# The sixteen-head stage gets its turned tokens by VectorE, DRAM and small loads instead of TensorE

## The reference

```python
y = x.reshape(b, t, nh, hs).transpose(0, 2, 1, 3)        # nh = 16 heads of hs = 16 features
scores = jnp.einsum('bhtk,bhsk->bhts', y, y) / math.sqrt(hs)
attn = jax.nn.softmax(scores, axis=-1)
o = jnp.einsum('bhts,bsc->bhtc', attn, x)                # every head sums the whole 256-feature tokens
o = o.transpose(0, 2, 1, 3).reshape(b, t, nh * c)
return o @ weight
```

## Time and profile before

| what | value |
|---|---|
| median of 3 runs | 3955.74 us (3955.32 to 3961.43) |
| profiled execution, first to last instruction | 3959.9 us |
| TensorE busy in it | 3751.7 us (95%) |
| VectorE, ScalarE, GpSimd busy | 67%, 57%, 55% |
| chain that ended last | 86% TensorE, 6% VectorE, 3% issue |
| sixteen-head stage | about 1373 us to 2670 us of the span |

### The profile page before, as it was taken

How to read it: one execution, slowest core, us unless ns; L and a number is a source line. 1 busy time by engine, 2 the same in 40 slices (tenths; PEclk the granted TensorE clock), 3 DMA queues, 4 the chain that set the end, 5 groups by cost and what they waited for, 6 DMA issues and landing times.

```text
span 3959.9 us, 75575 instructions
## 1 busy us (share of the span) xinstructions
PE 3751.7 (95%) x23552; PEld 3069.5 (78%) x23552; DVE 2649.7 (67%) x7350; ACT 2237.8 (57%) x5232; POOL 2192.4 (55%) x2179
## 2 busy tenths in 40 slices
PE   4999999999999799999999999998999999999997
PEld 3777777777777688888888888886777777777776
DVE  6677777777777465555555555656777777767774
ACT  2666665567656455444444444445656765567564
POOL 3465565555555355555555555654555555555553
PEclk8999999999999899999999999999999999999999
DMA  4000001110010100000000010001010011100110
GB/s 142 16 31 28 19 19 53 48 36 24 30 31 29 46 28 22 1 17 7 12 17 2 17 44 1 17 1 52 20 35 22 19 41 50 39 30 24 34 32 25
DMA packets 119063, 114.72 MB, mean 29 GB/s; under 512 B 13181, under 2 KB 116233, under 8 KB 118793
## 3 DMA queue, kind: packets, MB, share of 16 engines
q1 hardware_dynamic: 118792, 111.44, 8.9%
HBM read 73.69 MB, written 29.36 MB: 26 GB/s over the span
## 4 chain that ended last, share of the span: by engine, by line
PE 86%; DVE 6%; issue 3%; ACT 2%; POOL 1%; DMA 1%; DVEq 0%; SPq 0%; ACTq 0%; POOLq 0%
PE psum L1366 21%; PE psum L1367 20%; PE psum L1368 20%; PE psum L1480 6%; PE psum L1490 5%; PE psum L1510 4%; PE psum L1469 3%; PE psum L1615 3%; PE psum L1563 1%; DVE probs L1065 1%; PE psum L1446 1%; PE psum L1427 1%; DVE turned_sin L1031 1%; DVE nT_lo L1127 1%; DVE ssq L1038 1%
## 5 line engine op out<-in xcount | busy, mean ns | idle before, releaser
L685 POOL TENSOR_TENSOR ge_lo<-ge,ge_hi 128x512 fp32r<-128x512 f32 x512 | 716.8, 1403 | 541.2 <-PE psum L1368 311.3
L885 ACT ACTIVATE ge<-psum 128x512 f32<-128x512 f32 x512 | 306.3, 598 | 623.7 <-PE psum L1615 611.8
L645 POOL TENSOR_SCALAR probs<-probs,rz 128x256 f32<-128x256 f32 (+1 forms) x1024 | 446.1, 456 | 354.6 <-DVE rz L1079 354.6
L1256 DVE CAST ge_hi<-ge 128x512 fp32r<-128x512 f32 x512 | 245.2, 480 | 537.5 <-ACT ge L885 531.4
L791 ACT ACTIVATE probs<-probs,nb,rq 128x256 f32<-128x256 f32 (+1 forms) x1024 | 575.1, 564 | 20.2 <-DVE nb L1073 17.1
L1065 DVE CUSTOM_DVE_ANT_0 probs<-psum,mask 128x256 f32<-128x256 f32 (+1 forms) x1024 | 339.3, 387 | 255.0 <-PE psum L1480 200.2
L627 POOL TENSOR_TENSOR rinv<-ssq,minus_half 128x16 f32<-128x16 f32 x124 | 376.1, 3033 | 126.6 <-DVE ssq L1042 123.2
L655 POOL TENSOR_TENSOR hid_lo<-gate,hid_hi 128x512 fp32r<-128x512 f32 x160 | 208.2, 1301 | 320.7 <-ACT hid_hi L823 320.7
L1366 PE MATMUL psum<-wqkv_hi,hT_hi 128*128 128x512 f32 x768 | 319.0, 415 | 5.9 <-DVE hT_lo L1016 3.4
L772 ACT ACTIVATE squares<-psum 128x512 f32<-128x512 f32 x256 | 153.2, 599 | 285.8 <-PE psum L1368 273.2
L622 POOL TENSOR_TENSOR turned_qk<-turned_qk,turned_sin 128x512 f32<-128x512 f32 x128 | 165.0, 1289 | 256.9 <-DVE turned_sin L1031 256.6
(11 more groups left out here) (163 smaller groups left out, 10650.0 us busy)
## 6 DMA issues: line engine op xcount, KB each, us to landing
xnext<-stream SPq DMA_DIRECT2D x32, 512.0 KB, 4.3
xmid<-stream SPq DMA_DIRECT2D x32, 512.0 KB, 3.8
stream<-xmid SPq DMA_DIRECT2D x16, 512.0 KB, 2.9
nrm<-xmid SPq DMA_DIRECT2D x32, 224.0 KB
wbuf<-L_ffn_wqkv SPq DMA_DIRECT2D x8, 768.0 KB, 8.2
wbuf<-L_ffn_w SPq DMA_DIRECT2D x8, 682.0 KB, 4.3
x_all<-L_attn_x SPq DMA_DIRECT2D x8, 512.0 KB, 7.6
stream<-x_all SPq DMA_DIRECT2D x8, 512.0 KB, 3.9
```

The costliest lines, as they stand in the source:

```text
L645: last = nc.gpsimd.tensor_scalar(pu, pu, rz[:, h, t:t + 1], 1.0, ALU.mult, ALU.mult)
L685: nc.gpsimd.tensor_tensor(ges[1][:, k % 4, :], ge[:, k % 4, :], f32(ges[0][:, k % 4, :]), ALU.subtract).then_inc(S["g_lo"], 1)
L885: nc.scalar.activation(ge[:, k % 4, :], RB[k % 2], ACT.Exp, scale=GSCALE, accum_out=gz[:, h, t:t + 1]).then_inc(S["g_exp"], 1)
L1256: V.tensor_copy(ges[0][:, k % 4, :], ge[:, k % 4, :]).then_inc(S["g_hi"], 1)
```

## The change

VectorE turns all tokens of a sequence once, in 32x32 blocks, hi and lo (`y_turn`, two instructions, at step 34 of the sequence before), into `y_blocks`. SyncE stores that to a DRAM tensor `y_turned` in 24 DMAs of 64 KB (`y_keep`), and loads each pair from there into `gaz` and `gaT` in 8 DMAs of 32 rows of 2 KB (`rows_in`), a pair ahead. `pack`, `turn_pair` and `turned` are gone, with their semaphores. The preparation of the first sequence moves from the drain into the last round of part one (`PREP_*`: `gs` statistics, `gn` normalise, `gh` and `gl` the hi and lo parts, `gv` the turning). The weight chunks of the first sequence are issued between the pairs.

```diff
+PREP_DVE = {"L4": "gs", "R7": "gn", "L7": "gl gv"}
+PREP_ACT = {"H7": "gh"}
+PREP_POOL = {"N6": "gp"}
...
+    y_turned = nc.dram_tensor("y_turned", (2, 2, 3 * GS, GH // 2, N), F32, kind="Internal").ap()
...
-    NEXT_ST, NEXT_VAR, NEXT_POW, NEXT_N, NEXT_HI, NEXT_LO = 24, 26, 26, 28, 30, 32
+    NEXT_ST, NEXT_VAR, NEXT_POW, NEXT_N, NEXT_HI, NEXT_LO, NEXT_TURN = 24, 26, 26, 28, 30, 32, 34
...
+        def y_keep(b, r):
+
+            need_apart(sp, (S["g_turn"], b + 1))
+            for slot, part in enumerate((0, 1, 0)):
+                for q in range(P // SQ):
+                    for odd in range(2):
+                        at = q * SQ + odd * GS
+                        kept = y_turned[r, odd, slot * GS:(slot + 1) * GS].rearrange("g f (t q c) -> g (f t) q c", t=NT, c=SQ)
+                        sp.dma_start(kept[:, :, q, :], y_blocks[at:at + GS, part].rearrange("p f t c -> p (f t) c")
+                                     ).then_inc(S["g_kept"], 16)
+
+        def rows_in(b, r, pp):
+
+            need_apart(sp, (S["g_kept"], KEPT * (b + 1)), (S["g_s"], G_STEPS * b + 8 * (pp - 1)))
+            for side in range(2):
+                both = y_turned[r, side, :, pp, :]
+                for at, first_row in ((gaz[pp % 2][side], 0), (gaT[pp % 2], GS)):
+                    for half in range(2):
+                        lo = side * P // 2 + half * 2 * GS
+                        src = both[half * first_row:half * first_row + 2 * GS, :]
+                        sp.dma_start(f32(at[lo:lo + 2 * GS, :]), src).then_inc(S[f"g_row{pp % 2}"], 16)
...
             def last(m, final, call=call):
+                if call == 0:
+                    y_keep(0, 0)
                 x_old(m, call)
                 if call == 0:
-                    need_apart(sp, (S["x_stored"], 16 * (B + 2)))
-                    for b in range(2):
-                        sp.dma_start(gx[b][:], tokens(x_mid[0], b)).then_inc(S["g_in"], 16)
+                    sp.wait_ge(S["pe_wo"], PAIRS * ROUNDS)
+                    rows_in(0, 0, 0)
                     for c in range(2):
                         w_g(c)
                 keep(m, True, call)
...
+                def rows_of(b, r, pp, which):
+                    rows_in(b, r, pp)
+                    if which == "first" and pp < G_CHUNKS - 1:
+                        w_g(pp + 1)
+
                 def sequence(b, r, which):
+                    rows_of(b, r, 1, which)
                     if which == "last":
                         x_ahead(ROUNDS, None)
                         w_qkv(2)
+                    rows_of(b, r, 2, which)
...
+                    for pp in range(3, 6):
+                        rows_of(b, r, pp, which)
+                    if which != "last":
+                        y_keep(b + 1, 1 - r)
+                    for pp in range(6, 8):
+                        rows_of(b, r, pp, which)
+                    if which != "last":
+                        rows_in(b + 1, 1 - r, 0)
...
-        def turned(b, pp):
-
-            act.wait_ge(S["g_t"], GH * b + 2 * pp + 1)
-
-            need(act, S["g_s"], G_STEPS * b + 8 * (pp - 1))
-            copy(gaz[pp % 2][0][half_rows[0], :], TB[0][half_rows[0], :])
-            copy(gaz[pp % 2][1][half_rows[1], :], TB[0][half_rows[1], :]).then_inc(S["g_tc"], 1)
-            act.wait_ge(S["g_t"], GH * b + 2 * pp + 2)
-            copy(gaT[pp % 2], TB[1]).then_inc(S["g_tc"], 1)
...
-        def pack(b, r, quarter):
+        def y_turn(b, r):
+
             dve.wait_ge(S["g_ylo"], b + 1)
-
-            need(dve, S["g_t"], GH * b + 4 * quarter)
-            cols = slice(quarter * 4 * GS, (quarter + 1) * 4 * GS)
-            for side, parts in enumerate(((0, 1, 0, 1), (0, 0, 1, 1))):
-                for c, part in enumerate(parts):
-                    last = V.tensor_copy(ga[:, side, :, :, c, :],
-                                         f32(gy[r][part][:, :, cols]).rearrange("p t (h g) -> p t h g", g=GS))
-            last.then_inc(S["g_pack"], 1)
+            need(dve, S["g_kept"], 16 * 3 * 2 * NT * b)
+            for part in range(2):
+                last = V.transpose(y_blocks[:, part].rearrange("p f t c -> p t f c"),
+                                   f32(gy[r][part]).rearrange("p t (f c) -> p t f c", c=SQ))
+            last.then_inc(S["g_turn"], 1)
...
-        def turn_pair(b, pp):
-            pe.wait_ge(S["g_pack"], 4 * b + pp // 2 + 1)
-            for side in range(2):
-                need(pe, S["g_tc"], GH * b + 2 * (pp - 1) + side + 1)
-                for t in range(NT):
-                    last = turn(TB[side][:, t * P:(t + 1) * P],
-                                ga[:, side, t, 2 * (pp % 2):2 * (pp % 2) + 2].rearrange("p h c g -> p (h c g)"),
-                                ident[:])
-                last.then_inc(S["g_t"], 1)
+        def rows_ready(b, pp):
+
+            pe.wait_ge(S[f"g_row{pp % 2}"], 16 * 8 * (GH // 4 * b + pp // 2 + 1))
...
                             if k % 8 == 0:
-                                pe.wait_ge(S["g_tc"], GH * b + 2 * (h // 2) + 2)
+                                rows_ready(b, h // 2)
```

More of the change, by code:

```diff
@@ L516, in a_round @@
             def a_round(n, prev=True, nxt=True, load=None, switch=None, final=0, layer=0, call=call):
+                if call == 0 and not nxt:
+                    need_apart(sp, (S["x_stored"], 16 * (B + 2)))
+                    for b in range(2):
+                        sp.dma_start(gx[b][:], tokens(x_mid[0], b)).then_inc(S["g_in"], 16)
                 if prev and final:
@@ L830, in some_steps @@
                     w_f(load, i)
+                if kind == "gh":
+                    y_hi(0, 0)
         def y_hi(b, r):
@@ L873, in sequence @@
                     for k in g_steps(which, TAIL):
-                        if k % 8 == 2 and k < G_STEPS:
-                            pp = k // 8 + 1
-                            if pp < GH // 2:
-                                turned(b, pp)
-                            elif which != "last":
-                                turned(b + 1, 0)
                         if k < G_STEPS:
@@ L1173, in some_steps @@
                     biases(load)
+                if kind == "gs":
+                    dve.wait_ge(S["g_in"], 16 * 2)
+                    statistics(0, gx[0], "g_st", "g_mv")
+                    variance(0, "g_mv", "g_var")
+                if kind == "gn":
+                    normalise(0, gn, gx[0], "g_rs", "g_y")
+                if kind == "gl":
+                    y_lo(0, 0)
+                if kind == "gv":
+                    y_turn(0, 0)
         def statistics(b, src, s_st, s_mv):
@@ L1226, in last @@
                     zeroed.then_inc(S["g_zero"], 1)
-                    dve.wait_ge(S["g_in"], 16 * 2)
-                    statistics(0, gx[0], "g_st", "g_mv")
-                    variance(0, "g_mv", "g_var")
-                some_steps(m + 1, True, False, -1, final=final, layer=1, part=slice(2, 3))
-                if call == 0:
-                    normalise(0, gn, gx[0], "g_rs", "g_y")
-                some_steps(m + 1, True, False, -1, final=final, layer=1, part=slice(3, 5))
-                if call == 0:
-                    y_lo(0, 0)
-                some_steps(m + 1, True, False, -1, final=final, layer=1, part=slice(5, 6))
-                if call == 0:
-                    dve.wait_ge(S["pe_p"], 2 * UNITS * ROUNDS)
-                    pack(0, 0, 0)
-                some_steps(m + 1, True, False, -1, final=final, layer=1, part=slice(6, None))
+                some_steps(m + 1, True, False, -1, final=final, layer=1, part=slice(2, None))
                 stage_end(dve, 1 + call)
@@ L1256, in sequence @@
                             V.tensor_copy(ges[0][:, k % 4, :], ge[:, k % 4, :]).then_inc(S["g_hi"], 1)
-                        if k % 16 == 4 and k < G_STEPS:
-                            quarter = k // 16 + 1
-                            if quarter < 4:
-                                pack(b, r, quarter)
-                            elif which != "last":
-                                pack(b + 1, 1 - r, 0)
                         c, _, kk = back(b, r, which, k, LAG_OUT)
@@ L1597, in sequence @@
                     for k in g_steps(which, TAIL):
-                        if k % 8 == 1 and k < G_STEPS:
-                            pp = k // 8 + 1
-                            if which == "last" and pp < GH // 2:
-                                done = " ".join(AHEAD_PE[j] for j in AHEAD_PE if j < k).replace("+", "").split()
-                                for name in done[-2:]:
-                                    read(name[0], int(name[1:]), ROUNDS, 0)
-                            if pp < GH // 2:
-                                turn_pair(b, pp)
-                            elif which != "last":
-                                turn_pair(b + 1, 0)
                         if k < G_STEPS:
```

47 lines of the change are left out of this document (22 added, 25 removed).

## The result

| | median | lowest to highest | runs |
|---|---|---|---|
| before | 3957.87 us | 3955.32 to 3961.43 | 4 |
| changed | 3905.99 us | 3903.55 to 3909.73 | 4 |

The ratio is 0.9863, 95% interval 0.9849 to 0.9877: the change takes off 51.9 us, where 55.4 were forecast. From here on "before" and "changed" are these two kernels. In the changed one the three products stand at L1395 to L1397, the score at L1624, the 32x32 transposes at L1254, the stores at L533 and the small loads at L545.

A forecast was written before the change was run, and what follows sets the result against it. TensorE was taken to bound the sixteen-head stage. Terms -54.8 - 1.7 - 7.7 + 4 + 6.3 - 1.5 sum to -55.4 us: 3900 us against the median 3955.74; range of 8 in 10, 3878 to 3975.

The forecast's parts named there:

- 63 groups of transposes: Stage: TensorE is spared eight transposes for each of 63 pairs, 0.87 us a group, 54.8 us in all.
- drain: first pair and `hid_lo`: Drain: the 64th pair's transposes go, 1.7 us; `hid_lo` on GpSimd without pack copies beside it, 2.0 us.
- start of the stage: ScalarE's copies, `w_lo`: After the barrier: first step, ScalarE's three copies go, 1.7 us; second, TensorE's `w_lo` wait and slow clock at step 4, 4.0.
- last round: Last round of part one: VectorE's added preparation costs 2 for statistics, 0.5 normalise, 1.1 the rest; 3.6, say 4 us.
- seven `y_turn`: Step 34: two VectorE transposes of 1.2 us delay the next cast; TensorE waits 0.9 us in 7 sequences, 6.3 us.
- waits for `ge_lo`: Stage: without pack copies, part of TensorE's 2.9 us of waits for `ge_lo` goes, 1.5 us gained.
- The third price of 1.1: Last round: `y_lo` and two transposes ahead of the last `oT_lo`, less VectorE's 2.76 us wait, cost some 1.1 us.
- The stores: Per sequence, 24 stores take 15.4 us of 22 available, issues 9.1 at 0.38 each; late from 0.92 us an issue.
- the 48 us of the rival: Stores of a sequence, if read-modify-write doubled a 512 B piece's 31 ns: 48 us, 26 late seven times, 4080 us.
- Late rows: Step 48: pieces at 47 ns make stores 36.1 us, rows 14.1 late in 7 sequences: 4002 us; chance 0.20 including doubled form.
- Transposes of 2.3 us: Smaller-gain rival: VectorE transposes at 2.3 us (+16) and rows late by 2 us each time (+14): 3930 us; chance 0.13.
- The chain taking the transposes' place: Stage: TensorE instead waits 0.87 us for `ge_lo` at each of 63 places; about 3953 us, no change; chance 0.05.

The follow-up runs named there:

- experiment 2: Changed kernel with eight unread identity transposes put back on TensorE at k%8 = 1 (59 groups): 3959.54 us, ratio 0.9991 to the kernel before.
- experiment 6: Changed kernel with every store of turned tokens issued twice, the second to a DRAM tensor nobody reads: 4052.98 us, ratio 1.0228 to the kernel before.
- experiment 9: Kernel before the change with one of the eight pack copies of a quarter left on VectorE: 3952.62 us, ratio 0.9972 to the kernel before.
- experiment 4: Changed kernel with the first sequence's statistics, normalise and parts at earlier steps of the last round of part one: 3905.59 us, ratio 0.9859 to the kernel before.
- experiment 3: Changed kernel with VectorE's two transposes at step 33 instead of 34: 3906.81 us, ratio 0.9854 to the kernel before.
- experiments 5: Changed kernel with VectorE's transposes at step 33 and the first preparation earlier in the last round: 3895.89 us, ratio 0.9831 to the kernel before.
- experiment 7: Changed kernel with stores in pieces of 512 B instead of 128 B, same bytes and number of stores: 3909.23 us, ratio 0.9862 to the kernel before.

## Why the prediction was right, and which terms were off

**Right.** TensorE bounded the stage, what it was spared came off the end, and the rows came in time. Both halves were turned around on the chip: with the transposes back the gain is gone (+50.6 us, experiment 2), with the rows late it turns into a loss (experiment 6).

**The terms of the sum.** Forecast -55.4, measured -51.9.

| term | forecast | measured | from |
|---|---|---|---|
| 63 groups of transposes | -54.8 | -54.0 | 2: 63 x 50.6/59 |
| drain: first pair and `hid_lo` | -3.7 | -4.8, -3.7 when run again | stretches; 9 gives -3.1 without the copies |
| start of the stage: ScalarE's copies, `w_lo` | -5.7 | about -2.3 | 9: -2.6; the stretch by itself -2.1 |
| last round | +4 | +4.6, +3.4 when run again | stretches; 4 takes off 2.8 to 4.0 |
| seven `y_turn` | +6.3 | +4.4 to 5.4 | 0.63 by starts; 3: 0.8 each |
| waits for `ge_lo` | -1.5 | 0 or above | 9: 2.9 us as before; 3: 4.8 us in 10 with `y_turn` at step 33 |

The largest miss is the start of the stage, 3.4 us. By the stretch itself its gain is 8.1 less the nine groups in it (6.6 us, experiment 2), plus one `y_turn` (0.6): 2.1 us. The forecast's first step there, ScalarE's three copies for 1.7 us, fails: they weren't on the path. GpSimd's three `ge_lo` after the barrier show it, changed kernel first, then before:

```profile
1371.65 4.13 POOL L741 TENSOR_TENSOR ge_lo<-ge,ge_hi 128x512 fp32r<-128x512 f32 x3 [8.94 <-DVE ge_hi L1289]
```

```profile
1378.21 2.72 POOL L685 TENSOR_TENSOR ge_lo<-ge,ge_hi 128x512 fp32r<-128x512 f32 x2 [11.42 <-DVE ge_hi L1256]
1381.29 1.27 POOL L685 TENSOR_TENSOR ge_lo<-ge,ge_hi 128x512 fp32r<-128x512 f32 x1 [0.36 <-DVE ge_hi L1256]
```

The third ends 9.77 us after the last residual's issue, and 9.99 before: taking the copies away freed 0.2 us, and then GpSimd, with three in a row, was next. In the second step, 4.0 us for `w_lo` was taken as if the whole wait went; 1.31 of 2.67 us stays, since the value that VectorE subtracts comes late in any case. I named the work that ended late, and didn't ask what is late next.

In the drain the sum left out the clock. TensorE's wait for `hid_lo` went from 2.69 us to 1.08: 1.6 of the 2.0 forecast. Behind the long wait the granted clock was 0.67 (1365.5 to 1368, before) and 0.56 (1368 to 1370); behind the short one it is 1.00 (1361.5 to 1366, changed), and so it is in experiment 9 (1361.8 to 1368), where the wait is 1.28. From the matmul behind the wait to the first score go 7.59 us before, 5.98 in experiment 9 with the same instructions, and 5.10 in the changed kernel. So 1.6 us came back with the clock, and the eight transposes are worth 0.9 and not the 1.7 of the chain, which was their price at the lowered clock (0.79 us between starts in experiment 9, 1.56 before). 1.6 + 1.6 + 0.9 = 4.1 us; the rest of the 4.8 isn't shown, since this stretch takes 50.9 to 53.4 us in the six profiles whose program is the same there but for the shape of the stores.

In the last round the forecast had 2 us for the statistics ahead of an `oT_lo`; the wait grew by just that (0.38 to 2.42 us). 0.5 for the normalise was too little: from that matmul to the one that waits for `pT` go 6.3 us in both profiles of the changed kernel, 4.9 before. The two make 3.4, which is what the second profile has. In the first the granted clock was 0.50 behind the second wait (1309 to 1312), which is where its 1.2 us more went; in the second it was lowered ahead of that wait (0.77 in 1307 to 1313), in time that TensorE would have waited in any case. The third price of 1.1 falls into the drain: TensorE waits there 1.39 us for the last `oT_lo` (at 1324.39; 0.71 when run again), and not at all before or in experiment 4.

`y_turn` cost 0.63 to 0.8 us and not 0.9. The cast was late by 1.0 us where the working had 1.2 (the two transposes and a cast take 2.64 us by starts, not 2.8), and the slack was 0.37, the upper of its two values: the lo part of step 34 ends at 2057.16 and its matmul starts at 2057.53.

**The stores.** 15.4 us was the sum of pieces on the engines, with 9.1 for the queue beneath it. Measured: 18.4, set by the queue; the pieces alone would need 10 to 12 (768 for each engine at 13.1 to 15.6 ns). One slip lies in the working of a piece: 542 large pieces at 47 ns are 25 us and not 32, so the small ones of the earlier trace rows come to 19 ns and not 16. The 20 ns taken are hardly touched by it. The mis-sized term is the issue, 0.38 us taken from 512 KB transfers, 0.77 in fact. It stayed under the stated limit of 0.92 and hence cost nothing, but nearer to it than the prediction told. The doubling behind the 48 us of the rival was the prediction's own assumption; no row showed it, and no store here does.

**The rivals.** Late rows: the mechanism exists, from 22.4 us on, and the stores missed it by 3.6 to 4.0 us. Transposes of 2.3 us: they take 1.2. The chain taking the transposes' place: the stage's waits for `ge_lo` are 7.9 us in 17, and 4.8 in 10 with `y_turn` at step 33 (experiment 3), and not 0.87 at each of 63 places.

## What to carry to other kernels

Where one engine is busy for 99% of a stage, its work can be priced by the distance of starts and taken at that price off the end; moving it to DRAM and back is then free as long as a queue's budget, counted from the step that makes the data to the step that needs it, holds. Count that budget in issues as well as in bytes and pieces, with the price of an issue of the same shape: of 24 stores the queue was the limit, of 12 the DMA engines were. And where a stall is taken away, write down what is late next before counting it: of the gains counted at the start of the stage one was 0.2 us of 1.7 and the other half or less. Look at the granted clock behind the stall too: in the drain it gave back as much again as the wait did.

## What the runs showed of the hardware that was not expected

- A store of 64 KB from 16 partitions takes 0.77 us of the issuing queue on the mean (0.57 at the shortest) with 512 pieces of 128 B, and 0.67 with 128 pieces of 512 B; one of 128 KB from 32 partitions 0.88 (0.59 at the shortest), with the DMA engines 92% busy; one of 512 KB from 128 partitions 0.40. The Trainium skill, "DMA: Bandwidth & Descriptors", Issuing engines are not separate DMA queues, calls the time to initiate a DMA usually small beside the DMA itself; here it was the limit, 0.77 us each on the queue against 2.9 to landing.
- Pieces of 128 B from SBUF to DRAM took 15.6 ns of a DMA engine with engines 65% busy and 13.1 ns at 92%; pieces of 512 B took 51 to 58.
- A 32x32 transpose of 128x1024 fp32 on VectorE takes 1.20 to 1.24 us, the same as `gy_lo` of that size.
- TensorE's granted clock was 0.50 to 0.71 over the 5 us behind each of the seven waits of 16.0 to 18.8 us in experiment 6 (0.50 is the lower of its two levels) and 0.93 to 1.00 in the next 5; a middle sequence lost 2.4 us beside the wait. In the drain it fell behind a wait of 2.69 us (0.67, then 0.56) and stayed at 1.00 behind waits of 1.08 and 1.28 us.
- Part three, with the same instructions everywhere, took 1283.1 to 1284.5 us in eight profiles, 1278.5 and 1278.9 in those of experiments 5 and 9, and 1287.3 in that of experiment 2. In 16 us at its change of layer the granted clock was 0.89 in 5 and 9 and 0.59 in six of the eight, 0.60 in experiment 2, 0.79 in the first profile of the changed kernel and in experiment 7. The medians of 5 and 9 lie lower than their edits explain, so it seems to belong to the kernel and not to one execution; that is inferred. It is 0.13% of the time, and only the stretches tell it from an edit's own effect.
